# Four moves in the order of a fused attention and routing loop

## What is computed

```python
# per sequence: x [256, 256], ctx [77, 512], 16 heads of 64
xn  = layernorm(x)
q   = split(xn @ Wq) * 64 ** -0.5
k,v = split(ctx @ Wkv)                     # one learned key and value ahead of the 77
att = softmax(q @ k.T) @ v                 # 16 heads x 256 rows x 78 keys
out = layernorm(att.reshape(256, 1024) @ Wout) * ln_scale + ln_bias
x1  = x + tanh(g_xattn) * out
# over all 8192 rows: 32 experts of width 128, 8 taken for each row, and a shared one
x2  = layernorm(x1)
aff = sigmoid(x2 @ Wr + br);  top_v, top_i = top_k(aff, 8);  w = top_v / sum(top_v)
y   = shared(x2) + sum_e w[:, e] * down_e(silu(gate_e(x2)) * up_e(x2))
return x1 + tanh(g_ffn) * y
```

## Time and profile before

| | |
|---|---|
| median of 3 executions | 2076.17 us (2074.87 to 2076.47) |
| the profiled execution's own time | 2093.39 us |
| its span | 2091.7 us |
| mean granted TensorE clock | 0.98 of full speed |
| busy share of the span: PE, DVE, ACT, POOL | 95%, 76%, 65%, 57% |
| instructions on PE, DVE, ACT, POOL | 14626, 3736, 3958, 1286 |
| indirect DMAs to the pages (L833) | 512, mean 1036 ns, 196.3 us idle before them |

### The profile page before, as it was taken

How to read it: one execution, slowest core, us unless ns; L and a number is a source line. 1 busy time by engine, 2 the same in 40 slices (tenths; PEclk the granted TensorE clock), 3 DMA queues, 4 the chain that set the end, 5 groups by cost and what they waited for, 6 DMA issues and landing times.

```text
span 2091.7 us, 43908 instructions
## 1 busy us (share of the span) xinstructions
PE 1982.2 (95%) x14626; PEld 1740.9 (83%) x14626; DVE 1599.2 (76%) x3736; ACT 1363.9 (65%) x3958; POOL 1202.1 (57%) x1286
## 2 busy tenths in 40 slices
PE   7999799999999999999987999999999989899995
PEld 7889688888888888888874788888888878788883
DVE  3422248888888888888877766679998888899997
ACT  3211277777777777777753377777776666677771
POOL 1322104777777777777766200047777777777776
PEclk9999899999999999999999999999999999999998
DMA  8664478766666666666666999999999999999997
GB/s 269 222 194 166 142 299 306 268 227 229 230 228 228 228 228 228 231 228 227 233 229 226 316 289 287 285 325 401 402 402 378 359 363 365 358 392 402 401 368 267
DMA packets 286181, 597.36 MB, mean 286 GB/s; under 512 B 54629, under 2 KB 158790, under 8 KB 285958
## 3 DMA queue, kind: packets, MB, share of 16 engines
q1 hardware_dynamic: 236806, 460.27, 62.4%
q0 software_dynamic: 49152, 134.28, 17.8%
HBM read 296.74 MB, written 297.66 MB: 284 GB/s over the span
## 4 chain that ended last, share of the span: by engine, by line
PE 55%; DVE 13%; DMA 11%; issue 4%; POOL 3%; ACT 2%; POOLq 0%; DVEq 0%; SPq 0%; ACTq 0%
PE ring L141 7%; PE sim L1233 6%; PE ring L1277 6%; PE ring L142 6%; PE ring L143 6%; PE ring L1295 5%; DMA w_raw<-in_experts 5%; DVE parts L1758 4%; DMA parts<-results_dram,kept_index 3%; POOL parts L1649 3%; DMA results_dram<-y 2%; PE xps L1855 2%; DVE wq_l L1720 2%; DVE up_ps L1809 2%; DVE w_l L1732 2%
## 5 line engine op out<-in xcount | busy, mean ns | idle before, releaser
L1649 POOL DMA_INDIRECT parts<-results_dram,kept_index x512 | 538.9, 1052 | 377.9 <-DMA results_dram<-y 218.7
L833 POOL DMA_INDIRECT pages_dram<-rows,kept_index x512 | 530.5, 1036 | 196.3 <-issue 143.3
L890 ACT ACTIVATE exps<-sim,minus_max 128x78 f32<-128x78 f32 x1024 | 316.1, 349 | 28.8 <-DVE minus_max L979 28.8
L1758 DVE SCALAR_TENSOR_TENSOR parts<-parts,kept_weight 128x256 f32<-128x256 f32 x448 | 213.6, 477 | 46.1 <-DMA parts<-results_dram,kept_index 43.9
L890 ACT ACTIVATION_READ_ACCUMULATOR exps<-sim,minus_max 128x1 f32 x1024 | 236.3, 231 | 0.0
L1701 ACT ACTIVATE hid_h<-up_ps 128x512 fp32r<-128x512 f32 x175 | 104.2, 596 | 180.0 <-DVE up_ps L1809 177.9
L1855 PE MATMUL xps<-ident,xin 128*128 128x128 f32 x1272 | 167.5, 275 | 30.2 <-DVE wq_l L1720 21.6
L141 PE MATMUL yps<-w_h,hid_h 128*128 128x256 f32 x636 | 179.6, 282 | 0.1
L143 PE MATMUL yps<-w_l,hid_h 128*128 128x256 f32 x636 | 179.0, 281 | 0.0
L142 PE MATMUL yps<-w_h,hid_l 128*128 128x256 f32 x636 | 178.5, 281 | 0.0
L1670 ACT ACTIVATE w_h<-w_raw 128x768 fp32r<-128x768 f32 x159 | 135.2, 851 | 61.1 <-DMA w_raw<-in_experts 60.8
(11 more groups left out here) (229 smaller groups left out, 5911.8 us busy)
## 6 DMA issues: line engine op xcount, KB each, us to landing
xin<-pages_dram SPq DMA_DIRECT2D x159, 512.0 KB, 8.4
results_dram<-y SPq DMA_DIRECT2D x159, 512.0 KB
w_raw<-in_experts SPq DMA_DIRECT2D x159, 385.0 KB
pages_dram<-blank SPq DMA_DIRECT2D x108, 512.0 KB
pages_dram<-blank SPq DMA_DIRECT2D x12, 1536.0 KB
keys_dram<-keys SPq DMA_DIRECT2D x16, 624.0 KB, 4.6
kT<-keys_dram SPq DMA_DIRECT2D x32, 312.0 KB
v<-values_dram SPq DMA_DIRECT2D x32, 308.0 KB
```

The costliest lines, as they stand in the source:

```text
L833: pool.indirect_dma_start(dram["pages"], bass.IndirectOffsetOnAxis(ap=kept_index[:, at:at + 1].bitcast(U32), axis=0), buffer(batch)[:, k / ...
L890: last = act.activation(exps[u % 2][:, h, :], scores(u)[:, h // 4, h % 4, :], ACT.Exp, bias=minus_max[u][:, h:h + 1], accum_out=row_sum[u] ...
L1649: pool.indirect_dma_start(parts[slot(batch, t)][:, k, :], None, done, bass.IndirectOffsetOnAxis(ap=kept_index[:, at:at + 1].bitcast(U32), ...
L1758: dve.scalar_tensor_tensor(out=out, in0=part[:, k, :], scalar=kept.weight[:, at:at + 1], in1=part[:, TOPK, :], op0=ALU.mult, op1=ALU.add). ...
```

## The change

Two products change places in `RING`, two groups of scores take another place among them, one routing step moves behind one eviction, and one group of VectorE's moves behind another. No instruction is added or removed.

```diff
-RING = ["X", "N2", "Oa", "T0a", "Ob", "T0b", ...]
+RING = ["X", "Oa", "N2", "T0a", "Ob", "T0b", ...]

 ROUTE_AFTER = {"T1a": ["logits", "top", "mask"], "PV0b": ["placed"], "Q3": ["opened", "page", "moved", "slot"],
-               "PV1a": ["key"], "PV1b": ["kept"]}
+               "PV1b": ["key", "kept"]}

 # VectorE
-                if name == "T0a" and 1 <= b <= B:
+                if name == "T0b" and 1 <= b <= B:
                     dve.wait_ge(ring_full, nth(RING, "Ob", b))
                     statistics(1, lambda t: bank("Ob", b)[:, t * D:(t + 1) * D], b - 1)

 # TensorE
                 if name == "Oa" and here:
                     similarity(2, b)
+                if name == "N2" and here:
                     similarity(3, b)
```

More of the change, by code:

```diff
@@ L84 @@
 VSLOTS = 2
-RING = ["X", "N2", "Oa", "T0a", "Ob", "T0b", "L", "T1a", "Q0", "T1b", "Q1", "PV0a", "PV0b", "T2a", "R", "T2b", "T3a", "Q2",
+RING = ["X", "Oa", "N2", "T0a", "Ob", "T0b", "L", "T1a", "Q0", "T1b", "Q1", "PV0a", "PV0b", "T2a", "R", "T2b", "T3a", "Q2",
         "T3b", "Q3", "PV1a", "PV1b"]
```

## The result

The changed kernel takes 2085.15 us (median of 21 executions) against 2076.01 us for the kernel before (21 executions beside it). The forecast was +11.1 us, 2087.3.

The account below looks back on a forecast made before the run. PE's own loop was taken as the bound, with a ring over GpSimd only 0.34 us shorter, which the change lengthens. Terms 13.2 - 0.5 - 1.6 = +11.1 us gave 2087.3 us, range 2066 to 2096.

Parts of the forecast that it names:

- two pass lengths: Attention loop: long passes of 26.69 us (+0.67) and short ones of 26.09 us (+0.07).
- The loops: Attention loop: PE's own work, and a ring through VectorE, GpSimd, ScalarE and PE, only 0.34 us shorter.
- the statistics come 1.08 us late: VectorE copies T0b first, so mean_var is ready at 606.12, not 605.04; less 0.34 to spare, +0.74 us a pass.
- The share of the two lengths: Attention loop: 9 of 27 passes short, 18 long, as before; the mixture costs +0.47 us a pass.
- The alternation of transposes and scores: Sim 3 behind N2 on PE: one more alternation costs 0.0 to 0.1 us; taken as 0.
- Oa's wait stays: PE at Oa: the wait of 0.34 us for low(PV1b) stays, since Oa and low(PV1b) both come earlier; 0 us.
- The first passes: Batches 1 and 2 have statistics but no scatters, so each gains 0.27 us: -0.5 us.
- The loop's end: Pass 32: Oa runs in PE's wait for ScalarE's rows; -1.6 us at L, -4.3 if the clock stays up.
- The rule of the Trainium skill: GpSimd contends with VectorE instructions with two SBUF inputs; by it alone every scatter meeting one is held.
- all passes long: Attention loop, second rival: every scatter beside weigh is held, 28 x 0.67 = 18.8; +16.7, 2092.9 us; chance 0.16.
- Rival 1: Attention loop: GpSimd has more room outside the profiled execution, PE stays the bound; -10.0, 2066.2 us; chance 0.20.
- the ring: Attention loop: VectorE's statistics, GpSimd's eight scatters, ScalarE's rows and exponentials, PE's sim 3, T0a, Ob; 0.34 us below PE's loop.

Follow-up runs that it names:

- e5: Kernel before with one more unused tensor_tensor (0.72 us on GpSimd) between the eight scatters and the shift; ratio 1.0048 to the kernel before.
- e2: Kernel before with only the statistics moved behind T0b; ratio 1.0044 to the kernel before.
- e1: Changed kernel with the statistics of the output rows back behind T0a, other three moves kept; ratio 1.0026 to the kernel before.
- e7: Kernel before with the statistics behind T0b and eight scatters ahead of the first make_rstd; ratio 0.9964 to the kernel before, 2068.87 us.
- e3: Changed kernel with eight scatters instead of seven ahead of the first make_rstd on GpSimd; ratio 0.9991 to the kernel before.
- e9: Changed kernel with eight scatters ahead of the first make_rstd, and sim 2 and sim 3 together behind N2; ratio 0.9956 to the kernel before.
- e10: Changed kernel with key back behind PV1a, ahead of low(PV1b); ratio 1.0045 to the kernel before.
- e4: Kernel before with eight scatters instead of seven ahead of the first make_rstd on GpSimd; ratio 0.9993 to the kernel before.

## Why the prediction was right

The mechanism of the loop was right, and so were its two pass lengths. That the sum came within 3 us of the time is in part luck, since two terms were too high and the time holds 3.8 us that no term had:

| us against the kernel before | forecast | traces |
|---|---|---|
| at X of pass 4 | -0.5 | -0.9 |
| 26 passes, to X of pass 30 | 26 x 0.47 = +12.2 | +9.2 |
| from there to L of pass 32 | 2 x 0.47 - 1.6 = -0.7 | -3.8 |
| sum at L of pass 32 | +11.0 | +4.5 |
| behind it, to the end (by the time of the runs) | 0 | +3.8 |

- **The loops.** "The second is only 0.34 us shorter": e5 measured 0.36. That the statistics come 1.08 us late and that all but this slack arrives at sim 3 gave passes of 26.69 and 26.09; measured 26.70 and 26.10, and in e2 without the other moves the same.
- **The share of the two lengths** was mis-sized. The forecast kept the 9 short of 27 of the kernel before (+0.47 a pass); the changed kernel had 13 short of 25 (+0.37). Over the 25 passes that is 9.3 instead of 11.8 us, 2.5 too many. Runs may differ by it: 17 executions of the changed kernel lie between 2077.9 and 2088.8 us, 17 of the kernel before between 2072.6 and 2076.9, those of e5, which has one length, between 2084.7 and 2087.2 (4 executions). But e1 and e7 have one length too and spread over 9 and 10 us, so that the share varies between runs is not shown; one trace was read of each kernel.
- **The alternation of transposes and scores** was wrong: "0 us, with 0.0 to 0.1" was 0.17 to 0.19 us (e1, e3, e9). The bound came from the first matmul of one group; at N2 there are two changes of kind. Part of the price is idle time ahead of the weight loads (15.4 us at the scores and 1.8 at N2 in e3, 12.9 and 0.0 in e9, from 411 to 991 us). It didn't show in the time, because PE waits at sim 3 by more than that: e2, with the old order, has passes of the same two lengths.
- **Oa's wait stays**: 0.34 forecast, 0.33 measured, 0.77 without the key's move (e10), as worked out.
- **The first passes**: -0.5 forecast; X of pass 4 starts 0.87 us earlier than before (359.14 against 360.01).
- **The loop's end**: from X of pass 30 to L of pass 32 the trace gives -3.8 us. The forecast has -1.6 in that place, with -4.3 if the clock stays up. The granted clock was 0.97 from 1085 to 1095 us and 0.86 from 1095 to 1105, where it had been 0.50, so only about the first half of Oa ran at the lower level (0.21 us a matmul against 0.12). The size isn't the order's alone: from X of pass 30 to L of pass 32 e10, with the same order, takes 61.2 us, no less than the kernel before, with a granted clock of 0.66 from 1095 to 1105 us, and e4, with the order before, takes 58.9. The changed kernel's rows:

```profile
1085.00:1095.00 10.00, 6.89 (x54) 4.88 (x55) 9.83 (x34) 4.63 (x8) 7.87 (x8) 0.97 0.48 175
1095.00:1105.00 10.00, 9.92 (x64) 9.09 (x65) 6.81 (x30) 2.13 (x5) 7.06 (x10) 0.86 0.43 122
```

- **The rule of the Trainium skill** (GPSIMD Engine Reference, Key points: VectorE instructions with two SBUF inputs contend with GpSimd) agrees with every held scatter here. Taken as "every scatter near `weigh` is held by it" it gave all passes long, +16.7 us. The trace has both forms: a scatter that starts under the last part of one such instruction may get in before the next.
- **Rival 1** (PE stays the bound outside the profiled execution) needed the ring 0.34 to 0.94 us shorter; the time of the runs, e2 and e5 exclude it. The 17.2 us between the first profiled execution and the median most likely lay in the expert phase: that trace has four dips of the clock there (25 us each at 0.87 to 0.93), while e4's passes, of the same order, have its length of 26.03 us, and the later spans without such an excess are 2061.6 to 2085.5.

What stays open are the 3.8 us behind the loop. At the first expert transpose (L1856) the changed kernel is 5.9 us late and at its end, by the runs, 8.3; for e1 these are 1.4 and 5.4, for e2 9.2 and 9.1. From L of pass 32 to that transpose it takes 89.2 us against 87.8, with a granted clock of 0.91 against 0.93 from 1100 to 1200 us, which would be about that much (an estimate from these two rows). From the transpose to the end of the span the traces without a dip of the clock in between take 887.4 us (changed), 888.3 (e1), 886.8 (e10), and with the order of before 887.5 (e2) and 890.1 (e5): no sign that the changed order costs anything there. The last 2 to 4 us of the changed kernel and of e1 aren't explained.

## What to carry to other kernels

A wait of an engine that is far from busy (GpSimd, 70.6 of 100 us in the loop) is not free time: look for the ring through it, add up its steps, and compare its length with the bound's before anything is put ahead of its start. When two or three loops have nearly the same length, single edits measure as nothing or as a loss and pay only together, as the statistics and the eighth scatter did (1.0044 and 0.9993 alone, 0.9964 together). An idle gap of the bound engine that goes away can come back at its next wait; take the gain only as far as the second-longest loop allows.

## What the runs showed of the hardware

- Four transposes put between two groups of scores cost PE 0.17 us more than the same transposes behind a group of products (25.93 against 25.76 us a pass, e3 and e9), and 0.18 to 0.19 more than beside other transposes (26.20 against 26.02, e1 and before; 25.93 against 25.74, e3 and e7).
- A scatter on GpSimd mostly takes 0.96 us. When VectorE works on `normalise`, `residual` or `weigh` at its start, whose two inputs both lie in SBUF, it ends 0.83 us after that instruction, whatever its own start was (0.82 to 0.85 in all 111 that were held in the kernel before and the changed one from 400 to 1000 us). Under VectorE's `centre` (L1009), one input of which lies in PSUM, it stays at 0.96: 23 of 23 in either kernel. Some 45 of the 366 scatters of that stretch of the changed kernel take 1.04 to 1.09 us with no such instruction beside them; why stays open.
- A scatter that starts under `residual`, 0.14 us before `weigh` begins (617.28 and 617.42), has two outcomes, 1.06 and 1.66 us, 0.83 behind the one instruction or behind the other, and a ring through it makes two lengths of a pass out of them.
